# Mixer: where in a chunk's round the norms of the next chunk and of the last are done

## The reference

```python
delta = shifted - x
z = jnp.tanh((x + delta * mu_x) @ W_x1.T).reshape(B, T, 5, lr)
mus = jnp.einsum('blnr,dnr->blnd', z, W_x2.reshape(D, 5, lr)) + x_bias
# r, w, k, v, g: five projections of x + delta * mu of its own
# w = -exp(tanh(..) @ B_w.T + b_w); per head, over the tokens:
#   o_t = q_t (S + u * k_t v_t);  S = exp(w_t) * S + k_t v_t
o = (o - mean) / jnp.sqrt(var + EPS)          # by head
o = o * gn_weight + gn_bias
o = o * jax.nn.silu(g)
return o @ W_o.T                              # added to the input
```

## Time and profile before

| | |
|---|---|
| Time, median of 3 runs (lowest, highest) | 3639.49 us (3636.15, 3640.57) |
| Profiled execution: time, span | 3638.03 us, 3636.2 us |
| Busy over the span: PE, DVE, ACT, POOL | 91%, 69%, 55%, 21% |
| Mean granted TensorE clock | 0.933 |
| Mixer | the first 866 us of the span |
| DVE busy in the mixer's round from 406.33 to 457.41 us | 35.2 of 51.1 us |

### The profile page before, as it was taken

One profiled execution on the slowest core, in us unless ns is written; L12 is line 12 of the kernel. 1 busy time (PEld: TensorE's weight loads), 2 busy tenths in 40 slices (PEclk: granted clock), 3 DMA queues, 4 the chain that ended last, 5 costly groups with the idle time before them and its releaser, 6 DMA issues. The chain is left out here.

```text
span 3636.2 us, 78012 instructions
## 1 busy us (share of the span) xinstructions
PE 3315.7 (91%) x31460; PEld 1957.4 (54%) x31460; DVE 2503.2 (69%) x4755; ACT 2009.9 (55%) x2991; POOL 758.0 (21%) x887
## 2 busy tenths in 40 slices
PE   7999999995899939999999999999999999968998
PEld 4556555554677714444444444444444444427777
DVE  6676667663677717777767778687786776807776
ACT  3444444441555503666666667666676666755554
POOL 3444444342121110102011020110110201011112
PEclk8888888885999966999999999999999999989999
DMA  1000000001111142122222212122121312120110
GB/s 49 14 25 25 13 25 25 19 13 60 61 47 47 36 93 39 25 43 50 38 37 51 42 46 43 28 59 42 46 42 23 65 33 44 22 74 30 49 51 30
DMA packets 110471, 145.76 MB, mean 40 GB/s; under 512 B 21632, under 2 KB 94352, under 8 KB 109328
## 3 DMA queue, kind: packets, MB, share of 16 engines
q1 hardware_dynamic: 109344, 137.95, 16.1%
q0 software_dynamic: 768, 2.82, 0.4%
HBM read 53.99 MB, written 38.41 MB: 25 GB/s over the span
## 5 line engine op out<-in xcount | busy, mean ns | idle before, releaser
L1767 DVE TENSOR_REDUCE b_half_max<-banks 128x1 f32<-128x512 f32 x2048 | 1314.4, 685 | 443.2 <-PE banks L1492 261.6
L1718 ACT ACTIVATE b_p_t<-banks 128x1024 f32<-128x1024 f32 x1024 | 1047.0, 1025 | 397.3 <-PE banks L1492 256.0
L1548 PE MATMUL banks<-b_k_stack,b_q_stack 62*128 62x512 f32 x2048 | 828.9, 477 | 34.2 <-issue 17.8
L1609 PE MATMUL banks<-b_q_stack,b_k_stack 64*128 64x512 f32 x2048 | 851.7, 469 | 0.0
L1564 PE MATMUL banks<-b_p_t,b_v 128*17 128x256 f32 x8192 | 640.9, 385 | 25.1 <-ACT b_pv L1687 24.5
L1609 PEld LDWEIGHTS banks<-b_q_stack,b_k_stack 64*128 64x128 f32 x2048 | 342.9, 185 | 432.2 <-issue 416.7
L1492 PE MATMUL banks<-b_tables,b_halves 64*128 64x128 bf16 x4096 | 437.0, 224 | 0.0
L1548 PEld LDWEIGHTS banks<-b_k_stack,b_q_stack 62*128 62x128 f32 x2048 | 337.5, 188 | 68.6 <-issue 25.4
L1108 ACT ACTIVATE ffn_relu<-banks,ffn_scale_fc 128x512 f32<-128x512 f32 x256 | 176.3, 689 | 274.2 <-PE banks L1044 274.2
L1057 PE MATMUL banks<-ffn_proj_t,ffn_r_hi 128*128 128x256 f32 x1024 | 257.0, 285 | 2.5 <-DVE ffn_r_lo L1227 2.5
L1564 PEld LDWEIGHTS banks<-b_p_t,b_v 128*17 128x17 f32 x8192 | 135.9, 95 | 225.3 <-issue 76.6
(11 more groups left out here) (231 smaller groups left out, 4948.1 us busy)
## 6 DMA issues: line engine op xcount, KB each, us to landing
ffn_x<-x SPq DMA_DIRECT2D x32, 512.0 KB, 3.9
b_q_stack<-b_qk_hi SPq DMA_DIRECT2D x256, 64.0 KB
b_k_stack<-b_qk_hi SPq DMA_DIRECT2D x256, 64.0 KB
a_x<-hidden_states SPq DMA_DIRECT2D x16, 512.0 KB, 3.9
x<-a_x SPq DMA_DIRECT2D x16, 512.0 KB, 2.9
x<-ffn_x SPq DMA_DIRECT2D x16, 512.0 KB, 2.9
b_x<-x SPq DMA_DIRECT2D x8, 1024.0 KB, 5.6
b_k_stack<-b_qk_lo SPq DMA_DIRECT2D x128, 64.0 KB
```

What stands on the lines that cost most here:

```text
L1548: last = pe.matmul(m, q_stack[rows, slot, qb * P:(qb + 1) * P], k_stack[rows, slot, half * BANK:(half + 1) * BANK], start=True, stop=not h ...
L1609: last = pe.matmul(out, k_stack[stack, slot, kb * P:(kb + 1) * P], q_stack[stack, slot, half * BANK:(half + 1) * BANK], start=True, stop=n ...
L1718: act.activation(p_t[use % P_BUFS][:, :, :], scores[use % 2], ACT.Exp, scale=slopes()[pair][0]).then_inc(p_made, 1)
L1767: dve.tensor_reduce(half_max[:, (pair + rg * PAIRS) * QB + qb, half:half + 1], misc.at["max", g, turn], axis=AX.X, op=ALU.max, negate=True ...
```

## The change

The same instructions are issued, at other steps. `normalize` has 14 steps in place of 7, `finish` 16 in place of 12. Moments and their reciprocal root are taken by functions of their own (`take_moments`, `take_rstd`): for chunk 0 at the start, for chunk c + 1 at the last step of `normalize(c)`, which is in the round before. The new places in the round: `xn` 0.46; transposes of `xn` 0.54 and 0.61; `delta` and `mixed_x` 0.75; z 0.82 and 0.89; moments of the chunk after 0.96. For `finish`: squares 0.34, sum 0.41, scaling 0.59, transposes 0.66, product with the gate 0.72, outputs from 0.78 to 0.97. `prepare` and `recur` stay where they are.

```diff
-        NORMALIZE, PREPARE, RECUR, FINISH = 7, 14, 8, 12
+        NORMALIZE, PREPARE, RECUR, FINISH = 14, 14, 8, 16
...
         def tensor(pe):
             def normalize(c):
                 xt = xn_t[c % 2]
-                yield
-                yield
+                for _ in range(7):
+                    yield
                 for kt in range(KT):
...
                     turn.then_inc(xn_turned, 1)
-                    if kt == 0:
-                        yield
+                    yield
                 yield
                 yield
                 for m in range(2):
...
                     yield
+                yield
...
             def finish(c):
                 o = o_bufs[c % 2]
-                for _ in range(4):
+                for _ in range(10):
                     yield
                 pe.wait_ge(o_scaled, c + 1)
...
-                for _ in range(3):
-                    yield
+                yield
+                yield
                 for i in range(CT):
...
         def scalar(act):
...
             def finish(c):
                 o = o_bufs[c % 2]
+                for _ in range(5):
+                    yield
                 act.wait_ge(o_made, CT * (c + 1))
...
                 act.activation(o_sq, o[:, :, :], ACT.Square).then_inc(o_squared, 1)
-                for _ in range(4):
+                for _ in range(5):
                     yield
...
         def vector(dve):
-            def normalize(c):
-                par, x = c % 2, xs[c % X_BUFS]
-                xt, delta = xn_t[par], deltas[par]
+            def take_moments(c):
+                x = xs[c % X_BUFS]
                 dve.wait_ge(x_in_sem[c % X_BUFS], 16 * (c // X_BUFS + 1))
...
                 last.then_inc(moments, 1)
-                yield
+
+            def normalize(c):
+                par, x = c % 2, xs[c % X_BUFS]
+                xt, delta = xn_t[par], deltas[par]
+                if c == 0:
+                    take_moments(c)
+                for _ in range(6):
+                    yield
                 dve.wait_ge(norm_scale, c + 1)
...
-                yield
-                yield
-                yield
+                for _ in range(4):
+                    yield
                 dve.wait_ge(xt_made, 2 * c + 2)
                 dve.wait_ge(carried, c + 1)
...
                 last.then_inc(mixed_x_made, 1)
-                yield
-                yield
+                for _ in range(3):
+                    yield
+                if c + 1 < CHUNKS:
+                    take_moments(c + 1)
                 yield
...
             def finish(c):
...
-                yield
+                for _ in range(6):
+                    yield
                 dve.wait_ge(o_squared, c + 1)
                 dve.tensor_reduce(rstd[:, :], groups(o_sq), axis=AX.X, op=ALU.add).then_inc(o_power, 1)
-                yield
-                yield
+                for _ in range(3):
+                    yield
                 dve.wait_ge(o_rstd, c + 1)
...
-                for _ in range(4):
+                for _ in range(3):
                     yield
...
         def gpsimd(pool):
...
+            def normalize(c):
+                xt = xn_t[c % 2]
+                if c == 0:
+                    take_rstd(c)
+                for _ in range(8):
+                    yield
...
+                if c + 1 < CHUNKS:
+                    take_rstd(c + 1)
+                yield
...
             def finish(c):
-                yield
+                for _ in range(6):
+                    yield
                 pool.wait_ge(o_power, c + 1)
...
-                for _ in range(4):
+                for _ in range(5):
                     yield
                 pool.wait_ge(o_t_made, 2 * c + 2)
```

More of the change, by code:

```diff
@@ L569, in finish @@
                                    bias=gn_b[:, kt:kt + 1]).then_inc(o_t_made, 1)
-                for _ in range(FINISH - 4):
+                for _ in range(FINISH - 10):
                     yield
@@ L755, in gpsimd, with take_rstd @@
         def gpsimd(pool):
-            def normalize(c):
-                xt = xn_t[c % 2]
+            def take_rstd(c):
                 pool.wait_ge(moments, c + 1)
@@ L832, in finish @@
                 pool.tensor_tensor(o_t[:, :, :], o_t[:, :, :], gate[c % 3][:, :, :], ALU.mult).then_inc(o_gated, 1)
-                for _ in range(FINISH - 5):
+                for _ in range(FINISH - 11):
                     yield
```

## The result

The changed kernel takes 3736.2 us (median of 4 runs, 3734.05 to 3739.6), the kernel before 3639.84 us on the same chip (4 runs, 3636.15 to 3640.57): ratio 1.0268 [1.0250, 1.0285], 96 us slower. The profiled execution took 3739.60 us with a span of 3737.8, against 3638.03 and 3636.2: 101.6 us between the spans.

A forecast was written before the change was run, and what follows sets the result against it. TensorE was taken to set the mixer's round. 14 rounds x 6.0 us (84), +2 at the start, 0 at the end, -3 for a vanished wait: +83 on 3638, so 3720 us; forecast 3700 to 3745 (0.62), 8-in-10 range 3675 to 3765.

The forecast's parts named there:

- The stall: TensorE waits before z for `mixed_x`, made behind VectorE's second gate product and tree level 3: 4.4 us a round.
- The clock behind it: Clock drops to half speed behind the wait for `mixed_x`: 2.0 us a round, bounds 0 and 7.8.
- rival (a): TensorE waits for `mixed_x`, but the clock does not drop behind it: 3692 us, chance 0.12.
- The gains: TensorE's early waits for VectorE shrink by 0.4 us a round; the 0.18 us wait at the first pair product vanishes.
- The first drop: The round's existing low-clock stretch, 13.6 us in the round shown, stays as long as before.
- rival (c): Relief of VectorE's early queue removes its wait and brings the clock back sooner: 3588 us, chance 0.10.
- The rounds' sum: Per round 4.4 + 2.0 - 0.4 = 6.0 us, over rounds 0 to 13: 84 us.
- The start: The two rounds of the start, bound by the tree of levels: its later place adds some 2 us.
- The end: Closing norm starts 1 to 2 us later, while round 14 loses waits of about that size: 0.
- Their durations stay: VectorE's moved pieces keep their durations, among them 2.6 us for the scaling of the output.

The follow-up runs named there:

- e7: Changed kernel with VectorE's ties turned so `normalize` goes ahead of `prepare`, and moments put behind the round's last step: 3649.7 us, ratio 1.0021 to the kernel before.
- e1: Changed kernel with only VectorE's `delta` and `mixed_x` moved two steps earlier, ahead of both gate products: 3661.4 us, ratio 1.0049 to the kernel before.
- e4: Changed kernel with four unused dense products added on TensorE ahead of its wait for `mixed_x`: 3689.6 us, ratio 1.0121 to the kernel before.
- e5: Kernel before with two unused dense products added on TensorE ahead of tile 1's pair product, in its `a_pair` wait: 3643.2 us, ratio 1.0001.
- e11: Kernel before with new `finish` steps, two unused products ahead of tile 1's pair product, and moments behind the round's last step: 3583.1 us, ratio 0.9834.
- e2: Kernel before with only the new 16 steps of `finish`, `normalize` as before: 3624.4 us, ratio 0.9967.
- e12: Kernel before with the new `finish` steps and moments behind the round's last step, without added products: 3634.1 us, ratio 0.9967.

## Why the prediction was right

The time, 3736, lies 16 us above the 3720 predicted, inside both ranges, by the mechanism that was predicted.

- **The stall.** 4.4 us predicted, 4.56 measured, in each round. Its parts agree as well: masking to gate product 4.49 (4.48), `delta` and `mixed_x` 2.6 (2.88), no new wait at the transposes of `xn` or `o`. That the order on a tie decides is shown by e7, and for `delta` alone by e1.
- **The clock behind it.** 2.0 predicted, 1.9 measured. The second drop lasts 5.5 us in the mean, TensorE is idle for 1.75 of them, and half of the rest is lost. From z's begin to the next round's mixes it is 10.2 us in the long round (735.61 to 745.77), of which 1.9 are lost to the clock, and 9.7 in the short one with 1.4 lost: 8.3 at full speed, where the prediction had 7.8. That the idle time brings this drop is shown by e4. The Trainium skill (TensorE: Matmul & The Clock Gate, section What's actually happening) says that the throttled state is the default and that activity releases it; e4 and e5 agree, where work in the idle time kept the clock up, and rival (a) falls. At the first drop the rows are not as plain: in round 1 of the kernel before the clock fell with TensorE recorded as busy up to it, but for 0.18 us in front of the round's first pair product.
- **The gains.** -0.4 and -0.2 a round predicted, and they came. Waits of PE from 115 to 760 us, in the kernel before and then in the changed one:

```profile
PE banks L359 <- ACT a_pair L531: 18.5, 12, 1.9
PE banks L392 <- DVE a_mix L631: 3.1, 6, 1.9
PE banks L418 <- DVE a_state L699: 2.6, 6, 0.7
PE banks L359 <- issue: 2.1, 12, 0.2
PE banks L396 <- DVE a_mix L631: 1.4, 6, 0.2
```

```profile
PE banks L271 <- DVE a_mixed_x L621: 50.1, 11, 4.6
PE banks L359 <- ACT a_pair L531: 19.8, 12, 1.9
```

Over rounds 1 to 13 the waits for mixes were 0.36 us a round, those for the state 0.21 and the one at the first pair product 0.18. All are gone, 0.75 in all; the wait for `a_pair` grew by 0.1.
- **The first drop.** 0 predicted ("as long as before"), 0.9 us a round measured: the term that was left out. Without TensorE's idle time in it, what it costs is 7.8 us a round instead of 6.9. So rival (c) falls at the clock, not at VectorE's waits: they went and the drop stayed. e5 shows why it looked possible: the relief is worth much more in a kernel whose clock stays up.
- **The rounds' sum.** 4.56 + 1.9 + 0.9 - 0.75 + 0.1 is 6.7, and the rounds are 6.67 us longer; TensorE's work, counted at full speed, is 42.1 us a round in both. The prediction had 5.8. Its two costs and its gains are right, one by one. What is missing in the whole sum, 18.6 us of the 101.6 between the spans against 83, is 11.4 in rounds 1 to 13, 4.2 in the start and 5.0 at the end, less 2.2 in round 0.
- **The start.** Mis-sized, a little. The two rounds of the start and round 0 were put down with +2 and 6.0. The first pair product comes at 59.7 us instead of 53.5, and round 0 takes 49.8 instead of 46.2: 9.8 where 8 was given for both. The start alone is three times its term, round 0 little more than half of its own.
- **The end.** 0 predicted. Round 14 takes 45.3 instead of 44.7, and what follows it adds 4.4 us. Of these, 3.4 lie ahead of the mixer's last output product, which begins 56.6 us behind the last round's first pair product instead of 53.2; 1.3 of them come from the last eight output products, of which more run at half speed (958.83 to 964.79 us, before 859.52 to 864.17).

The account between the two spans, 101.6 us: 6.2 before the first pair product, 3.6 in round 0, 86.8 in rounds 1 to 13 (13 x 6.67), 0.6 in round 14, 4.4 behind.

**Open.** What starts the first drop and what decides how long it lasts. It was 10.2, 13.7, 17.1, 20.5 or 23.9 us in kernels whose work in that stretch hardly differs, and by turns in one and the same kernel. That two dense products in the wait for `a_pair` halve the low time is shown (e5). But a wait isn't needed for a drop: in e11 TensorE idles 0.2 us a round, and 11 of the 13 rounds still have one of 6.8 us, right behind the pair products of tile 1 (a window of e11, TensorE busy all through):

```profile
627.00:633.80 6.80, 6.80 (x26) 2.86 (x22) 5.93 (x15) 2.05 (x7) 1.41 (x1) 0.50 0.00 0
```

Why the first drop is 1 us longer in the changed kernel, with less of VectorE's work in it, and what of e2's gain is the clock's, is not shown.

## What to carry to other kernels

Where a producer moves to a later place in an in-order queue, read what stands ahead of it there down to the order on a tie: here `delta` had its inputs some 9 us before it ran, and stood behind a gate product that happened to be listed first; TensorE waited 4.56 us for it. An idle time in front of a consumer can cost twice, once itself and once in the clock behind it (4.56 and 1.9 us here), so a few dense products thrown away in it can be worth more than work saved elsewhere. And when removing a bound moves nothing, look for a second one at the same height before the idea is dropped: fill alone 0, relief alone -12 (e2 and e12), both together -60 us (e11).

## What the hardware showed beside this

The scaling of the output, the same instruction with 1024 columns, takes 2.58 us in the kernel before and 1.22 in most rounds of the changed one (columns of this view of one line: duration in ns as least, median and most).

```profile
L732 DVE TENSOR_TENSOR a_o<-a_o,a_rstd x16: 1218/1218/1628, 138.7 to 952.2; 128x1024 f32<-128x1024 f32 x16
```

In the kernel before it runs beside an addition of GpSimd's. Timelines of the kernel before, GpSimd and then VectorE:

```profile
424.00 2.00 POOL L784 TENSOR_TENSOR a_mix<-a_mix,a_xn_t 128x1024 f32<-128x1024 f32 x1 [2.18 <-DVE a_mix L631]
```

```profile
424.49 2.58 DVE L722 TENSOR_TENSOR a_o<-a_o,a_rstd 128x1024 f32<-128x1024 f32 x1
427.00 0.27 DVE L701 SCALAR_TENSOR_TENSOR a_state<-a_state,a_decay,banks 128x64 f32<-128x64 f32 x1
```

GpSimd's ends at 426.00, and VectorE's, begun at 424.49, ends 1.07 us later, at 427.07, about its own 1.22 us: as if it had stood still until GpSimd was through. The Trainium skill (SBUF — State Buffer, section SBUF: two separate sides) says that a VectorE instruction with two SBUF inputs and a GpSimd one that reads SBUF exclude each other, whichever comes second being blocked; the rows agree. No run here tries it by itself. The prediction kept 2.6 us for the moved scaling ("Their durations stay"), 1.4 too much; it lay beside other work, so the sum didn't change.
